# Sums of four steps for the softmax denominators in four more quarters of a decoder layer

## The chip, the cores and the metric

The kernel runs as one program on 1 core of a Trainium2 chip. The metric is the device time of one execution in microseconds (us), lower is better. The kernel before took 1848.51 us (median of 3 runs, 1848.01 to 1848.87).

## What is computed

One post-norm decoder layer in float32 on 2 x 1024 tokens of width 512: linear attention, cross-attention over 2 x 2048 context rows, and a mixture of 8 experts with the 2 best taken per token. The change touches the cross-attention alone:

```python
dots = jnp.einsum('bhnd,bhmd->bhnm', q, k) * SCALE     # 16 heads of 32, n = 1024, m = 2048
attn = jax.nn.softmax(dots, axis=-1)
out = jnp.einsum('bhnm,bhmd->bhnd', attn, v)
```

The kernel computes exp(score - shift), sums its products with v (the numerators) and sums it over m (the denominators), and divides once at the end.

## The kernel before, in words

**Turns, steps, blocks, quarters.** The cross-attention is a loop of 16 turns (0 to 15). A turn is a group of four heads for one half (512) of one batch item's queries. A turn has 16 steps; a step is 128 context rows. Two steps make a block, so a turn has blocks 0 to 7, and four steps make a quarter, so it has quarters 0 to 3 (quarter q is blocks 2q and 2q + 1). In one pass of the inner loop TensorE (PE) computes the eight score products of the next block (`score`, L1446) interleaved with eight products whose maxima are wanted for a later turn (`max_scores`, L1427), then now and then a piece of other work (rows of the output projection, L1258, L1358, routing tables L1258), then the numerators of the current block (`numerators`, L1457: 2 steps x 4 heads, which the trace shows as 16 records, two for each float32 matmul), and last whatever denominator sums are due (`denominators_of`, L1481). In what follows a block's window reaches from the start of its numerators to the start of the next block's numerators, and so holds its numerators, the denominator sums due in it and the score and maximum products that follow.

**The probabilities and how they are summed.** ScalarE (ACT) writes exp of each score into one of nine tiles `probs`, each [128, 4, 512] (L2207). GpSimd (POOL) adds the second step of each block onto the first, one head at a time (`add_head`, L2329, four additions a block). From there are two ways:

- A plain quarter: TensorE multiplies each pair's sum with a matrix of ones as soon as it is due, one block later. That is one sum of four matmuls (8 records) for each block, two for the quarter.
- A quarter by fours: GpSimd issues one accumulating DMA of 1 MB (`add_four`, L2333), which adds the first pair's sum onto the second pair's, and TensorE multiplies only that, four blocks later (three in the quarters of `LAST_BEFORE_PLAIN`). That is one sum of four matmuls for the quarter.

**A visit.** All denominator sums of a turn that are due in the same block make one visit: they accumulate in one PSUM bank, VectorE (DVE) turns the result once (`turn_den`, L1815, a transpose of 128x512) and GpSimd adds the turned column onto `den_s` (`add_den`, L2355 for the first of a turn, L2358 after). So two sums in one visit cost TensorE twice and VectorE and GpSimd once. The visit in which the last step of the turn is summed must be the turn's last; after it come the reciprocal (L1827), a transpose (L1828) and the division on GpSimd (L2367).

The program writes its order out by hand. What is due when is decided here:

```python
if not by_fours(turn, s):
    pending.append((clock + 1, turn, s + 1))
elif s % FOUR == 2:
    fours.append((turn, s + 1))
    pending.append((clock + (3 if (turn, s // FOUR) in LAST_BEFORE_PLAIN else 4), turn, s + 1))
```

`clock` counts blocks. Before the change the quarters by fours are: all four of turns 0 to 6 and 8; the first three of turns 7, 9 and 11; the second and third of turn 10; the first two of turns 13 and 14. Turn 12 has none and turn 15 has none. 47 quarters go by fours and there are 62 visits.

**The order on the other engines.** VectorE takes the maxima of the products of L1427 (`take_max`, L1793, eight a block) in the order in which TensorE makes them, and between them the transposes and the element-wise work of the output rows and the routing (L1870, L1896 to L1982). Maxima, denominator sums and side work take turns in a ring of four PSUM banks, so TensorE can be at most some four products ahead of VectorE. Score products use a ring of three banks which ACT frees. ACT's exp for a step waits for the numerators and for the addition that read the buffer it overwrites: the second tile of a pair five steps later, the first tile thirteen steps later (for a quarter by fours its DMA must have landed by then). On GpSimd the DMA of a quarter stands in the order after the additions of its second block and the divisions that are due, and before the additions of the next block. SyncE issues all loads of keys, queries and values.

Of the kernel before, what the change touches and what calls it, by code (L numbers as in the profile page):

```python
# [20 lines left out]
NG = H // HG  # L21
# [34 lines left out]
TILES_Y = 2  # L56
FOUR = 4

LAST_BEFORE_PLAIN = {(2 * NG - 1, 2), (9, 2), (10, 2), (11, 2)}

LATER_FOURS = {(8, 0), (8, 1), (8, 2), (8, 3), (9, 0), (9, 1), (9, 2), (10, 1), (10, 2), (11, 0), (11, 1), (11, 2),
               (13, 0), (13, 1), (14, 0), (14, 1)}
PARTS = 3
PIECES_Y = B * NT // TILES_Y
HALF_Y = B * NT // 2
# [73 lines left out]
def program(nc, t):  # L139
    ctx = ExitStack()  # L140
    with ctx:
# [178 lines left out]
        def by_fours(t, s):  # L320

            return t * MT + s < B * NG * MT - FOUR or (t, s // FOUR) in LATER_FOURS

# [549 lines left out]
        def add_denominators():  # L873
            while summed:
                t, s = summed.pop(0)
                do("add_den", t, s)
                if s == MT - 1:
                    divisions.append((t, WHOLE))
# [87 lines left out]
        for turn, (n, h) in enumerate(turns):  # L966
            b, g = groups[n]
            stay = stay_of[turn]
            for s in range(0, MT, 2):
# [49 lines left out]
                if not end:  # L1019
# [9 lines left out]
# [3 lines that stand above are left out]
                add_denominators()  # L1032
# [1671 lines left out]
```

## Time and profile before

| | before |
|---|---|
| median of 3 runs (lowest, highest) | 1848.51 us (1848.01, 1848.87) |
| the profiled execution: time of the run | 1852.36 us |
| the profiled execution: span | 1850.6 us |
| TensorE matmul busy | 1824.5 us, 99% |
| VectorE busy | 1275.9 us, 69% |
| ScalarE busy | 879.0 us, 47% |
| GpSimd busy | 845.6 us, 46% |
| mean granted TensorE clock | 0.994 of full speed |

The profiled execution took 1852.36 us, of which the span in the trace is 1850.6 us. Durations are read from that execution. Matmul records overlap, so a busy TensorE is not one that could not be quicker; what a group of matmuls costs is read from the chain of work that ended last, which gives each group the time by which it moves the end. "L1481" is line 1481 of the kernel.

### The profile page before, as it was taken

The numbers are of one execution on the slowest core, as the hardware profiler recorded it, in microseconds if no ns is written. First come the engines' busy times: TensorE is split into PE (matmuls) and PEld (weight loads), VectorE is DVE, ScalarE is ACT, GpSimd is POOL, SyncE is SP. The second block draws the span as 40 slices with busy tenths as digits, with TensorE's granted clock in tenths as the row PEclk, the third lists the DMA queues.
The fourth block names the chain that finished last, engine by engine and source line by source line (L and its number), as shares of the span: only waits on it lengthen the run. The fifth ranks groups of instructions, "written<-read, shape, count | busy, mean of one in ns | idle before, by whom it ended". The sixth has DMA issues, their size and how long they took to land.

```text
span 1850.6 us, 27558 instructions
## 1 busy us (share of the span) xinstructions
PE 1824.5 (99%) x10260; PEld 1275.2 (69%) x10260; DVE 1275.9 (69%) x2350; ACT 879.0 (47%) x1587; POOL 845.6 (46%) x817
## 2 busy tenths in 40 slices
PE   9999999999999999999999999999999999999998
PEld 8786687788655555555555545555459988899986
DVE  6775574268788788888799788779554455554457
ACT  4312322322666566666465556547635333344343
POOL 4002201100598899999687768667202223212232
PEclk9999999999999999999999999999999999999999
DMA  8003534584768586757596556444227766666744
GB/s 291 24 1 119 178 104 172 206 241 152 167 142 183 109 188 143 168 124 170 105 224 146 140 142 148 115 108 110 92 97 222 196 169 153 173 181 177 205 111 157
DMA packets 151286, 280.07 MB, mean 151 GB/s; under 512 B 14288, under 2 KB 50400, under 8 KB 145056
## 3 DMA queue, kind: packets, MB, share of 16 engines
q1 hardware_dynamic: 134896, 205.92, 37.8%
q0 software_dynamic: 16256, 72.39, 19.3%
q8 instruction: 81, 1.33, 0.3%
q14 instruction: 53, 0.43, 0.1%
HBM read 157.63 MB, written 71.60 MB: 124 GB/s over the span
## 4 chain that ended last, share of the span: by engine, by line
PE 87%; DVE 9%; DMA 2%; issue 1%; POOL 0%; ACT 0%; SPq 0%; POOLq 0%; ACTq 0%; DVEq 0%
PE banks L1258 37%; PE banks L1575 12%; PE banks L1446 12%; PE banks L1457 11%; PE banks L1427 11%; DVE max L1793 5%; PE banks L1481 4%; PE banks L1264 1%; DMA k_half<-in_xwk_t 0%; PE banks L1358 0%; DVE den_t L1815 0%; DMA y_rows<-y_nat 0%; POOL x_nat L2340 0%; DMA x_rows<-x_nat 0%; PE banks L1435 0%
## 5 line engine op out<-in xcount | busy, mean ns | idle before, releaser
L2329 POOL TENSOR_TENSOR probs<-probs,probs 128x512 f32<-128x512 f32 x464 | 585.3, 1308 | 185.7 <-PE banks L1457 184.5
L2207 ACT ACTIVATE probs<-banks 128x512 f32<-128x512 f32 x1024 | 518.4, 623 | 285.2 <-PE banks L1446 284.9
L1793 DVE TENSOR_REDUCE max<-banks 128x1 f32<-128x512 f32 x1024 | 625.3, 679 | 39.4 <-PE banks L1427 38.9
L1427 PE MATMUL banks<-k_stack,q_stack 98*128 98x512 f32 x1024 | 401.4, 400 | 3.9 <-DVE max L1793 3.9
L1446 PE MATMUL banks<-q_stack,k_stack 98*128 98x512 f32 x1024 | 404.6, 408 | 0.1
L1446 PEld LDWEIGHTS banks<-q_stack,k_stack 98*128 98x128 f32 x1024 | 191.6, 188 | 152.8 <-issue 103.7
L1457 PE MATMUL banks<-probs,v_grp 128*32 128x512 f32 x2048 | 252.3, 605 | 0.0
L1427 PEld LDWEIGHTS banks<-k_stack,q_stack 98*128 98x128 f32 x1024 | 193.0, 188 | 54.0 <-DVE max L1793 21.1
L1457 PEld LDWEIGHTS banks<-probs,v_grp 128*32 128x32 f32 x2048 | 60.3, 110 | 117.8 <-issue 111.5
L2271 ACT ACTIVATE hid<-banks,b1c 128x640 f32<-128x640 f32 x64 | 50.9, 796 | 189.6 <-PE banks L1575 189.6
L2021 DVE TENSOR_TENSOR hid_lo<-hid,hid_hi 128x640 fp32r<-128x640 f32 x64 | 52.7, 824 | 120.1 <-ACT hid_hi L2276 115.1
L2387 POOL DMA_INDIRECT y_rows<-eo,tok x35 | 60.9, 1739 | 162.1 <-DMA y_rows<-eo,tok 94.0
L2340 POOL TENSOR_TENSOR x_nat<-x_nat,bxo_row 128x512 f32<-128x512 f32 x16 | 21.3, 1358 | 232.7 <-PE banks L1264 232.7
L1258 PE MATMUL banks<-w_hi,hid_lo 128*128 128x512 f32 x320 | 126.5, 395 | 0.0
L1258 PE MATMUL banks<-w_lo,hid_hi 128*128 128x512 f32 x320 | 126.0, 394 | 0.0
L1258 PE MATMUL banks<-w_hi,hid_hi 128*128 128x512 f32 x320 | 125.1, 391 | 0.0
L1575 PE MATMUL banks<-xe_hi,w_hi 128*128 128x320 f32 x512 | 118.7, 309 | 0.0
L1575 PE MATMUL banks<-xe_hi,w_lo 128*128 128x320 f32 x512 | 118.6, 309 | 0.0
L1575 PE MATMUL banks<-xe_lo,w_hi 128*128 128x320 f32 x512 | 118.6, 309 | 0.0
L2378 POOL DMA_INDIRECT xg<-x_rows,tok x40 | 39.2, 981 | 161.7 <-DVE banks L1998 130.8
L1815 DVE STREAM_TRANSPOSE den_t<-banks 128x512 f32<-128x512 f32 x62 | 44.3, 715 | 75.9 <-PE banks L1481 71.8
L1481 PE MATMUL banks<-probs,ones 128*32 128x512 f32 x656 | 87.2, 603 | 2.1 <-DVE max L1793 2.0
(272 smaller groups left out, 2789.6 us busy)
## 6 DMA issues: line engine op xcount, KB each, us to landing
probs<-probs POOLq DMA_DIRECT2D x47, 1024.0 KB, 10.6
k_stack<-k_parts SPq DMA_DIRECT2D x144, 256.0 KB, 5.5
w_raw<-in_w_rows SPq DMA_DIRECT2D x8, 2048.0 KB, 9.9
w_raw<-in_L_ffn_w SPq DMA_DIRECT2D x8, 2048.0 KB, 8.5
q_stack<-q_parts SPq DMA_DIRECT2D x48, 256.0 KB
v_grp<-v_rows SPq DMA_DIRECT2D x48, 256.0 KB, 3.8
slot_rows<-xg SPq DMA_DIRECT2D x35, 256.0 KB, 2.1
xg<-slot_rows SPq DMA_DIRECT2D x140, 64.0 KB, 8.1
```

The lines of the kernel that those rows point to most:

```text
L1258: done = nc.tensor.matmul(out, lhsT, rhs, start=start and n == 0, stop=stop and n == len(operands) - 1)
L1427: nc.tensor.matmul(out, queries_of(t)[:, j, tile_of(k)], keys_of(t)[0:STK + SHIFT, j, mc * HALF:(mc + 1) * HALF], start=True, stop=True) \
L1446: nc.tensor.matmul(out, keys_of(t)[0:STK + SHIFT, j, tile_of(s)], queries_of(t)[:, j, :], start=True, stop=True).then_inc(scored.sem, 1)
L1457: done = nc.tensor.matmul(bank(NUM)[j * DH:(j + 1) * DH, :], v_grp[:, s, j * DH:(j + 1) * DH], probs_of(t, s)[:, j, :], start=s == 0, stop ...
L1481: done = nc.tensor.matmul(out[j * DH:(j + 1) * DH, :], ones[:, 0:DH], tile[:, j, :], start=begun and n == 0, stop=n == len(tiles) - 1 and ...
L1575: done = nc.tensor.matmul(both[:, h, 0:HC], w, x[:, h * HC:(h + 1) * HC], start=n == 0, stop=n == len(terms) - 1)
L1793: V.reduce_max(max4[:, tiles_of(t), :, :][:, k, j, mc:mc + 1], bank(bank_of["max", t, mc, k, j]), AX.X) \
L2021: V.tensor_tensor(hid_lo[:, f, :], hid[f % 2][:, :], hid_hi[:, f, :].bitcast(F32), ALU.subtract) \
L2207: S.activation(probs_of(t, s)[:, j, :], bank(bank_of["score", t, s, j]), ACT.Exp, scale=SCALE) \
L2271: S.activation(hid[f % 2][:, :].rearrange("p (h n) -> p h n", h=2), pairs[first][:, :, 0:HC], ACT.Gelu, bias=b1c[:, e, f:f + 1]).then_inc( ...
L2329: G.tensor_tensor(a[:, j, :], a[:, j, :], b[:, j, :], ALU.add).then_inc(pair_added.sem, 1)
L2387: G.indirect_dma_start(out=y_rows, in_=eo[turn % EO][:, :], in_offset=None, compute_op=ALU.add, out_offset=bass.IndirectOffsetOnAxis(ap=to ...
```

## The change

Four quarters join the set that goes by fours: (10, 0), (12, 0), (12, 1) and (13, 2). Since quarter 3 of turn 13 stays plain, (13, 2) also joins the set whose sum is due one block earlier, so that it shares the turn's last visit.

```diff
-LAST_BEFORE_PLAIN = {(2 * NG - 1, 2), (9, 2), (10, 2), (11, 2)}
+LAST_BEFORE_PLAIN = {(2 * NG - 1, 2), (9, 2), (10, 2), (11, 2), (13, 2)}
 
-LATER_FOURS = {(8, 0), (8, 1), (8, 2), (8, 3), (9, 0), (9, 1), (9, 2), (10, 1), (10, 2), (11, 0), (11, 1), (11, 2),
-               (13, 0), (13, 1), (14, 0), (14, 1)}
+LATER_FOURS = {(8, 0), (8, 1), (8, 2), (8, 3), (9, 0), (9, 1), (9, 2), (10, 0), (10, 1), (10, 2), (11, 0), (11, 1), (11, 2),
+               (12, 0), (12, 1), (13, 0), (13, 1), (13, 2), (14, 0), (14, 1)}
```

The denominator sums due in each block follow from the rule above (q0 is quarter 0; a quarter that is plain has an a for its first block's sum and a b for its second's; x8 is one sum, x16 two; blocks not named hold none):

| turn | before | after |
|---|---|---|
| 10 | block 1: q0a x8; 2: q0b x8; 7: q1 and q3a x16; block 0 of turn 11: q2 and q3b x16 | block 5: q0 x8; 7: x16; block 0 of turn 11: x16 |
| 12 | blocks 1 to 6: q0a, q0b, q1a, q1b, q2a, q2b, x8 each; 7: q3a x8; block 0 of turn 13: q3b x8 | block 5: q0 and q2a x16; 6: q2b x8; 7: q1 and q3a x16; block 0 of turn 13: x8 |
| 13 | block 5: q0 and q2a x16; 6: q2b x8; 7: q1 and q3a x16; block 0 of turn 14: q3b x8 | block 5: q0 x8; 6: none; 7: x16; block 0 of turn 14: q2 and q3b x16 |

## Rows read from the trace of the kernel before

**Rows 1.** Page, busy time of the engines, and chain that ended last by engine.

```profile
PE 1824.5 (99%) x10260; PEld 1275.2 (69%) x10260; DVE 1275.9 (69%) x2350; ACT 879.0 (47%) x1587; POOL 845.6 (46%) x817
...
PE 87%; DVE 9%; DMA 2%; issue 1%; POOL 0%; ACT 0%; SPq 0%; POOLq 0%; ACTq 0%; DVEq 0%
```

**Rows 2.** Windows of six blocks: length, busy time of each engine, clock, DMA share, GB/s.

```profile
1024.07:1030.67 6.60, 6.60 (x42) 3.61 (x41) 5.48 (x10) 4.01 (x9) 5.99 (x8) 1.00 0.83 219
...
1141.95:1149.14 7.19, 7.19 (x41) 3.29 (x41) 7.12 (x15) 4.62 (x10) 5.95 (x7) 1.00 0.15 36
1149.14:1156.56 7.42, 7.13 (x41) 3.34 (x40) 7.35 (x14) 4.02 (x9) 6.23 (x8) 1.00 0.47 108
1156.56:1166.33 9.77, 9.27 (x58) 5.12 (x57) 9.46 (x18) 4.48 (x10) 5.56 (x7) 1.00 0.22 49
1166.33:1172.96 6.63, 6.63 (x42) 3.61 (x41) 4.03 (x8) 3.38 (x8) 5.22 (x5) 1.00 0.38 87
...
1232.48:1238.22 5.74, 5.74 (x37) 3.33 (x29) 4.60 (x9) 3.38 (x8) 5.29 (x5) 1.00 1.03 227
```

**Rows 3.** Chain that ended last in turns 10, 12 and 13: start, us, what.

```profile
1025.99 0.86 PE banks L1481 x8
...
1070.56 1.72 PE banks L1481 x16
...
1168.25 0.86 PE banks L1481 x8
...
1240.33 1.72 PE banks L1481 x16
...
1247.79 0.86 PE banks L1481 x8
```

**Rows 4.** The same chain in blocks 1 to 3 of turn 12.

```profile
1145.69 0.60 DVE den_t L1815
...
1153.09 0.62 DVE den_t L1815
...
1160.52 0.04 DVE top L1800
...
1160.66 0.70 DVE den_t L1815
...
1164.38 2.01 PE banks L1258 x16
```

**Rows 5.** Timeline of block 3 of turn 12, on ACT and PE.

```profile
1160.91 3.99 ACT L2207 ACTIVATE probs<-banks 128x512 f32<-128x512 f32 x8
...
1163.83 0.46 PE L1427 MATMUL banks<-k_stack,q_stack 98*128 98x512 f32 x1
```

**Rows 6.** Chain in block 7 of turn 13 and block 0 of turn 14, with one DVE row.

```profile
1253.60 2.47 DVE L1793 TENSOR_REDUCE max<-banks 128x1 f32<-128x512 f32 x4
...
1254.37 1.89 PE banks L1481 x16
...
1263.02 0.90 PE banks L1481 x8
1264.10 0.72 DVE den_t L1815
```

**Rows 7.** The DMA of four steps, all 47: min/median/max ns on POOL; us to landing.

```profile
L2333 POOL DMA_DIRECT2D probs<-probs x47: 807/872/942, 494.4 to 1290.3; - x47
...
DMA to landing us min/median/max: 6.9/10.6/14.7
```

**Rows 8.** POOL and the chain around quarter 2 of turns 11 and 13.

```profile
1120.22 0.87 POOL L2333 DMA_DIRECT2D probs<-probs  x1 [0.25 <-POOL den_s L2355]
...
1136.42 1.76 PE banks L1481 x16
...
1244.61 0.20 POOL L2355 COPY den_s<-den_t 128x16 f32<-128x16 f32 x1
```

**Rows 9.** DVE's routing addition with two inputs in SBUF: min/median/max ns.

```profile
L1904 DVE TENSOR_TENSOR rt_lg<-rt_lg,router_bias x4: 191/1232/1241, 953.3 to 1373.1; 128x32 f32<-128x32 f32 x4
```

## The prediction

> **What bounds the kernel now.** I read the page first: TensorE is busy 99% of the span, and the chain of work that ended last is 87% TensorE, 9% VectorE [rows 1]. So work taken off TensorE counts in most places and not in all, and the question is what bounds each block in which a sum is removed. For that I cut turns 10, 12 and 13 into blocks by the starts of their numerators and asked for the windows of the blocks, then for the chain over the same stretches. The granted clock is 1.00 in all these windows [rows 2], the full 2.4 GHz level, and TensorE has no idle stretch in them that the change would lengthen, so no term for the clock is set.
>
> Three kinds of block are seen [rows 2]. The bare one, 1232.48 to 1238.22, holds eight scores, eight maxima and the numerators and no sum: 5.74 us, TensorE busy throughout, VectorE 4.60. The one with one sum, 1024.07 to 1030.67, is 6.60, that is 5.74 + 0.86; and the chain gives such a sum 0.86 and a double one 1.72 [rows 3]. There TensorE sets the time. The third kind is blocks 1 to 3 of turn 12, from 1141.95 to 1166.33: VectorE is busy 7.12 of 7.19, 7.35 of 7.42 and 9.46 of 9.77, because the routing work of other rows falls there, and the chain runs through VectorE, its transposes included [rows 4].
>
> **The change part by part.** A quarter by fours has one sum in place of two. Four quarters: four sums fewer, 4 x 0.86 = 3.44 us of TensorE. By the table of sums due, 12 sums' places change and the visits fall from 4 to 3 in turn 10, from 8 to 4 in turn 12 and from 4 to 3 in turn 13: six transposes fewer, 6 x 0.72 = 4.3 us of VectorE [rows 6], and six small additions fewer on GpSimd (0.2 each, as the last row of [rows 8]). Added are four accumulating DMAs, 0.87 us of issue on GpSimd and 10.6 us to landing each [rows 7]. The gain has to be placed block by block.
>
> Turn 10: blocks 1 and 2 lose a sum each, block 5 gains one. TensorE sets all three. Would VectorE take over? In block 2 it is busy 5.48, less 0.72 for its transpose is 4.76, under 5.74 [rows 2]: no. So -0.86 - 0.86 + 0.86 = **-0.86**.
>
> Turn 12, blocks 1 to 3: three sums and three transposes go, but VectorE sets the time, so the sums are worth nothing and the transposes what the chain gives them: 0.60 and 0.62 in blocks 1 and 2 [rows 4]. In block 3 the transpose is 0.70 of chain, but another limit lies close beneath: the exps of that block start at 1160.91, just after VectorE's top (1160.52), since ACT's copy of that maximum stands ahead of them in its order, and with three score banks TensorE's last maximum product starts only at 1163.83 [rows 5] and would end about 1164.1, against 1164.38 at which the tables' products start [rows 4]. That chain is not shortened by the transpose behind it. It leaves about 0.3. Stretch: -0.60 - 0.62 - 0.31 = -1.53. Block 4 (6.63, one sum, VectorE 4.03 [rows 2]) is TensorE's: -0.86. Blocks 5 and 7 gain a sum: +1.72. Together **-0.67**, against -1.72 by TensorE's count.
>
> Turn 13: block 5 goes from a double sum to one and block 6 from one to none: -1.72 [rows 3]. In block 7 the double sum stays, at 1254.37; its bank is the one read by the fifth maximum, which VectorE finishes at 1253.60 + 0.61 = 1254.2 [rows 6]. VectorE came to it through the steps of a reciprocal root that it runs between its maxima, and it moves earlier with the transpose taken out, by some 1.3 to 1.6, while TensorE would be there 1.72 earlier: I put 0.25 of waiting there. In block 0 of turn 14 one sum becomes two: +0.86; but its transpose began at 1264.10, 0.18 after the sum's end at 1263.92, because VectorE was still at routing work [rows 6]. That wait is covered now: -0.18. Together -1.72 + 0.25 + 0.86 - 0.18 = **-0.79**. From that transpose on the chain is VectorE's for some 13 us, so its start is what counts.
>
> GpSimd: the four issues of 0.87 stand ahead of the next block's pair additions. The tightest place is block 2 of turn 12: GpSimd is busy 6.23 [rows 2], + 0.87 - 0.22 = 6.9 in a block that shrinks to 6.8. Its additions would lag by about 0.1 us, and ACT needs them only in the next block's exps. Price taken: 0; what hides it is about half a block of slack, and without that cover it would cost at most its own 0.87 once. SyncE's queue is not passed by anything: the DMAs are GpSimd's.
>
> The landings: three of the new quarters have over 20 us from issue to sum. The tightest is (13, 2). GpSimd frees itself at 1244.8 [rows 8], and the sum falls after the numerators of block 0 of turn 14, which start 1.44 earlier than now: about 1261.5. That is 16.7 us, against 14.7 for the slowest of 47 landings [rows 7]. The like case exists: quarter 2 of turn 11 is issued at 1120.22 and summed at 1136.42, 16.2 us later, and TensorE goes straight from its numerators into that sum [rows 8]. Price 0.
>
> A term that I can bound only is the meeting of VectorE and GpSimd. VectorE's small routing addition takes 0.19 us at its fastest and 1.23 in the median of four [rows 9], an excess of 1.04, near the length of one of GpSimd's additions. As the blocks move against each other, such meetings come and go in the stretches where VectorE sets the time. I take 0 for it, as the nearest rows show it on both sides of the change alike, and keep -1.0 and +2.0 (two places at which one may appear, at 1.04 each) for the range. The Trainium skill has a rule for it (SBUF — State Buffer, the section "SBUF: two separate sides"): VectorE and GpSimd share a pair of ports under an exclusive lock, so an operation of VectorE with two SBUF inputs waits for a whole GpSimd instruction. The trace agrees, 0.19 against 1.23 us; by that rule the gain in turn 12 could be lost to the new order, and it is the rival of the lock below.
>
> Sum: -0.86 - 0.67 - 0.79 = -2.32 us. After turn 14 nothing differs, and the end of the kernel is one chain of TensorE, routing and expert products, so the gain reaches the end. The profiled execution of 1852.36 (span 1850.6) would be 1850.04. It stood 3.85 above the median of the timed runs, 1848.51; the same difference off that median gives 1846.19, rounded **1846.2 us**, -0.13%. A measurement of this kernel tells about 0.2%, 3.7 us, from no change.
>
> **The rivals.**
>
> *TensorE's price in full.* VectorE turns out to have room where I saw it bind, with 4.3 us of transposes gone, and all four sums count: -3.44, 1845.1. For it: TensorE's 99%. Against: VectorE's 7.12 of 7.19 in turn 12. Chance 0.15.
>
> *The lock.* In the stretch of turn 12, or at the routing of turns 13 and 14, one or two operations of VectorE now meet GpSimd's additions: -2.32 + 1.04 = -1.3 with one, -0.2 with two, 1847.2 to 1848.3. For it: in blocks 1 and 2 of turn 12 VectorE's table work would come up to 1.2 us earlier against GpSimd's additions, which follow the numerators. Against: it can as well be lifted. Chance 0.22.
>
> *A large gain.* The full price and a meeting lifted: -3.44 - 1.04 = -4.5, 1844.0. Chance 0.07.
>
> *Slower: the landing of (13, 2).* Its DMA lands later than 16.7 us after issue and TensorE waits in block 0 of turn 14. It decides the sign from 16.7 + 2.3 = 19.0 us on; at 20.3 the time is +1.3, 1849.8. For it: one quarter more lies in flight beside the keys' and queries' loads. Against: 14.7 is the maximum of 47. Chance 0.06.
>
> That the change doesn't do what it says is no rival: both sets are constants that the plan reads.
>
> **How the numbers follow.** My case, -1.6 to -3.1, gets 0.50 with 1846.2 in its middle. The range takes it, the full price and nearly all of the lock, with some 0.4 us on either side for the spread of runs: 1844.5 to 1848.5. Faster by over 0.2% (under 1844.8) needs the large gain or the lucky edge of the full price: 0.09. Slower by over 0.2% (over 1852.2) needs a landing 6 us too late or several meetings: 0.03. The rest, 0.88, is within 0.2%.
>
> **What would show it.** In the profile after: 51 DMAs of four steps, 56 transposes L1815, 624 records of L1481; blocks 1 and 2 of turn 10 at 5.74 to 5.8 us and block 5 0.86 longer; blocks 1 to 3 of turn 12 at about 6.6, 6.8 and 9.5, still full on VectorE; a span of about 1848.3. Blocks 1 to 3 of turn 12 at 5.8, 5.8 and 7.8 would prove the first rival and me wrong about VectorE; a routing operation of 1.2 us where there was none the second; a wait of L1481 for a DMA in block 0 of turn 14 the fourth. A gain above 3.7 us or a loss would show that the method of adding blocks misses a coupling between them.

## The result, and the profile after

The changed kernel took 1857.03 us (median of 20 runs, 1850.94 to 1865.98) against 1848.97 us of the kernel before (20 runs, 1845.54 to 1852.50): ratio 1.0047, 95% interval 1.0037 to 1.0056. It is slower, where the prediction had 1846.2 and a range of 1844.5 to 1848.5. The profiled execution took 1855.75 us, span 1854.0, against 1852.36 and 1850.6.

Busy time by engine and the chain by engine, from the page of the changed kernel:

```profile
PE 1817.0 (98%) x10228; PEld 1275.3 (69%) x10228; DVE 1284.1 (69%) x2344; ACT 879.8 (47%) x1587; POOL 846.9 (46%) x815
...
PE 86%; DVE 10%; DMA 2%; issue 1%; POOL 1%; ACT 0%; SPq 0%; DVEq 0%; POOLq 0%; ACTq 0%
```

Against [rows 1], TensorE has 32 records fewer and VectorE 6. Yet VectorE is busy 8.2 us longer, though six transposes of 0.72 us are gone. That is the first sign: some of its operations took much longer. ("VectorE busy" holds the time in which an operation has begun and waits.)

The counts came as forecast (51 DMAs, 56 transposes, 624 records), and the landings did not suffer. Lines L2333, L1815 and L1481 of the changed kernel:

```profile
L2333 POOL DMA_DIRECT2D probs<-probs x51: 817/871/947, 494.2 to 1297.2; - x51
...
DMA to landing us min/median/max: 6.9/10.2/14.7
...
L1815 DVE STREAM_TRANSPOSE den_t<-banks x56: 704/717/718, 513.7 to 1365.4; 128x512 f32<-128x512 f32 x56
...
L1481 PE MATMUL banks<-probs,ones x624: 592/592/617, 512.4 to 1364.8; 128*32 128x512 f32 x156
```

Blocks 1 and 2 of turn 10, block 2 of turn 12 and block 2 of turn 14 of the changed kernel (windows: length, busy time of PE, PEld, DVE, ACT, POOL, granted clock, DMA share, GB/s):

```profile
1014.34:1020.09 5.75, 5.75 (x34) 3.34 (x33) 4.23 (x9) 3.35 (x7) 4.51 (x4) 1.00 0.40 107
1020.09:1025.83 5.74, 5.74 (x33) 3.34 (x32) 4.87 (x9) 4.02 (x9) 5.74 (x8) 1.00 1.04 281
1144.63:1159.30 14.67, 9.04 (x34) 5.40 (x33) 14.53 (x18) 4.82 (x9) 7.16 (x9) 0.65 0.59 126
1276.52:1290.61 14.09, 8.33 (x38) 5.41 (x37) 13.77 (x17) 4.73 (x9) 7.09 (x9) 0.76 0.37 74
```

Turn 10 is as predicted: 5.75 and 5.74 where [rows 2] has 6.60 for the second. But block 2 of turn 12 takes 14.67 us in place of 7.42 [rows 2], and block 2 of turn 14 takes 14.09 in place of 9.33. Block by block, the profiled executions differ so:

| | before | after | measured | predicted |
|---|---|---|---|---|
| turn 10, blocks 1, 2, 5 | 6.62, 6.60, 9.64 | 5.75, 5.74, 10.49 | -0.88 | -0.86 |
| turn 12, block 1 | 7.19 | 6.59 | -0.60 | -0.60 |
| turn 12, block 2 | 7.42 | 14.67 | +7.25 | -0.62 |
| turn 12, block 3 | 9.77 | 7.70 | -2.07 | -0.31 |
| turn 12, blocks 4, 5, 7 | 6.63, 6.81, 10.24 | 5.78, 7.63, 11.10 | +0.83 | +0.86 |
| turn 13, blocks 5, 6 | 7.65, 6.58 | 6.81, 6.07 | -1.35 | -1.72 |
| turn 13, block 7 | 8.64 | 9.93 | +1.29 | +0.25 |
| turn 14, blocks 0, 1 | 6.62, 6.74 | 7.45, 6.55 | +0.64 | +0.68 |
| turn 14, block 2 | 9.33 | 14.09 | +4.76 | 0 |

Blocks 1 to 3 of turn 12 go together, since VectorE's second table pass (L1970 to L1976), which ran over the start of block 3 before, now lies inside the long block 2: together +4.58 us where I had -1.53. Of the other blocks from turn 10 on, all but two are as before to 0.04 us. The table adds up to +9.9 us and the spans differ by 3.4 only, because the profiled execution of before had stretches at half the clock of its own: one ahead of turn 10 (600.62 to 607.45, granted clock 0.50; in the changed kernel turn 10 starts 3.1 us earlier), and one in block 7 of turn 14 and block 0 of turn 15 (10.17 and 7.19 us against 9.29 and 4.81 after). A third lies inside block 2 of turn 14 (1279.88 to 1283.29), so its 9.33 us are more than usual; with quarter (10, 0), (12, 0) or (12, 1) alone by fours this block took 8.66 to 8.67. What happened in block 2 of turn 12 is in the timelines of the changed kernel, VectorE first, then GpSimd, then TensorE (start, us, instruction, in brackets the idle time before it and its releaser):

```profile
1145.61 0.31 DVE L1972 TENSOR_TENSOR hot_col<-col_no,slot_col 128x160 f32<-128x160 int32 x1
1145.96 5.51 DVE L1974 TENSOR_TENSOR hot_col<-hot_col,weight 128x160 f32<-128x160 f32 x1
1151.51 0.46 DVE L1976 TENSOR_TENSOR hot_col<-hot_col,token_no 128x160 f32<-128x160 f32 x1
```

```profile
1145.09 0.84 POOL L2333 DMA_DIRECT2D probs<-probs  x1
1145.89 4.99 POOL L2329 TENSOR_TENSOR probs<-probs,probs 128x512 f32<-128x512 f32 x4
1150.78 1.00 POOL L2367 TENSOR_TENSOR heads_t<-num_c,den_c 128x128 f32<-128x128 f32 x2
```

```profile
1146.49 0.50 PE L1446 MATMUL banks<-q_stack,k_stack 98*128 98x512 f32 x1
1152.62 0.80 PE L1427 MATMUL banks<-k_stack,q_stack 98*128 98x512 f32 x1 [5.63 <-DVE max L1793]
1153.22 0.63 PE L1446 MATMUL banks<-q_stack,k_stack 98*128 98x512 f32 x1
...
1158.34 0.63 PE L1446 MATMUL banks<-q_stack,k_stack 98*128 98x512 f32 x1
```

VectorE's L1974, an operation of 0.32 us where nothing is in its way (the row behind this paragraph, from the kernel before), comes 0.07 us after the first of GpSimd's four additions and ends 5.51 us later, when all four and the first of two divisions are over. The maxima stand behind it, so TensorE waits 5.63 us for a bank. And then TensorE runs on at 0.43 us from one product to the next, where the bare block of [rows 2] leaves (5.74 - 1.92) / 16 = 0.24, 1.92 being its numerators' row: the granted clock of that window is 0.65, so a good part of it was at the lower of the two levels, 1.2 GHz. From 1152.62 to 1159.30 it makes 15 products in 6.7 us, where 3.6 is usual (15 x 0.24). The wait costs twice.

```profile
1150.01 0.32 DVE L1974 TENSOR_TENSOR hot_col<-hot_col,weight 128x160 f32<-128x160 f32 x1
```

Turn 14 has the same with the third operation of L1928, on VectorE and on GpSimd of the changed kernel:

```profile
1277.42 6.22 DVE L1928 TENSOR_TENSOR before<-before,rt_ms 128x8 f32<-128x8 f32 x3
```

```profile
1277.00 0.85 POOL L2333 DMA_DIRECT2D probs<-probs  x1
1277.77 5.03 POOL L2329 TENSOR_TENSOR probs<-probs,probs 128x512 f32<-128x512 f32 x4
```

In both places the DMA issue of four steps ends as the additions begin (1277.00 + 0.85 = 1277.85, additions from 1277.77): no gap. The kernel before has that DMA of turn 14 too, but there a gap of 0.12 us follows (1274.74 + 0.85 = 1275.59, additions from 1275.71), and VectorE's L1933 waits for one addition, 1.24 us. The additions wait for the first step's numerators and start some 1.25 us after the block does, before and after (1274.45 to 1275.71, 1276.52 to 1277.77); what moved is the issue, which starts 0.29 us into the block before and 0.48 us after, and so eats the gap. GpSimd and VectorE of the kernel before:

```profile
1274.74 0.85 POOL L2333 DMA_DIRECT2D probs<-probs  x1
1275.71 4.98 POOL L2329 TENSOR_TENSOR probs<-probs,probs 128x512 f32<-128x512 f32 x4
```

```profile
1275.76 1.24 DVE L1933 TENSOR_TENSOR before<-before,rt_ms 128x8 f32<-128x8 f32 x1
```

Theory of the port: a two-input operation of VectorE (two inputs in SBUF) that comes at the additions waits for one of them as a rule, but for the whole burst when a DMA issue of GpSimd ends straight into it. Rivals: the removed sums cost by themselves; the burst alone, without the DMA, does it; the DMA does it, gap or no gap.

### The profile page after: what moved, and what is told of

Same layout as the page of the kernel before. It is cut to its first block, busy times and chain, and to the rows that moved or that the text cites. A ratio compares the mean times of both kernels' runs of the same rounds, so it can differ in the third digit from the quotient of the medians.

```text
span 1854.0 us, 27469 instructions
## 1 busy us (share of the span) xinstructions
PE 1817.0 (98%) x10228; PEld 1275.3 (69%) x10228; DVE 1284.1 (69%) x2344; ACT 879.8 (47%) x1587; POOL 846.9 (46%) x815
## 4 chain that ended last, share of the span: by engine, by line
PE 86%; DVE 10%; DMA 2%; issue 1%; POOL 1%; ACT 0%; SPq 0%; DVEq 0%; POOLq 0%; ACTq 0%
PE banks L1258 36%; PE banks L1575 12%; PE banks L1446 12%; PE banks L1457 11%; PE banks L1427 11%; DVE max L1793 5%; PE banks L1481 4%; DMA raw<-in_x_t 1%; PE banks L1264 1%; PE banks L1358 1%; DMA k_half<-in_xwk_t 0%; DVE before L1928 0%; DVE den_t L1815 0%; DVE hot_col L1974 0%; POOL x_nat L2340 0%
## 5 line engine op out<-in xcount | busy, mean ns | idle before, releaser
L1781 DVE TENSOR_TENSOR out_lo<-banks,out_hi 128x512 fp32r<-128x512 f32 x48 | 33.0, 690 | 79.0 <-ACT out_hi L2152 78.8
L1815 DVE STREAM_TRANSPOSE den_t<-banks 128x512 f32<-128x512 f32 x56 | 40.1, 717 | 68.8 <-PE banks L1481 63.9
```

## The experiments

All ratios are against runs of the kernel before on the same chip, with 95% intervals.

### One quarter at a time

```diff
-               (13, 0), (13, 1), (14, 0), (14, 1)}
+               (13, 0), (13, 1), (14, 0), (14, 1), (12, 0)}     # or (10, 0), (12, 1), (13, 2)
```

For (13, 2) the quarter is in the other set too, as in the change.

> Only quarter (10, 0) goes by fours in addition. Its DMA is issued in block 2 of turn 10, where VectorE has no routing work. Theory of the port (GpSimd's divisions, DMA issue and four additions run without a gap, and a two-input VectorE operation that comes to them waits for nearly the whole burst, 5 to 6 us): no such meeting here, so -0.9 us (blocks 1 and 2 at 5.75, block 5 0.86 longer). Rival, that merging or removing sums costs through the banks or the visits: slower by 1 us or more here too.

> Only quarter (12, 0). Theory of the port: block 2 of turn 12 has L1974 at about 5.5 us in place of 0.33 and is some 7 us longer, net +4 to +7 us. Rival, that the shift of the blocks by all four quarters together makes the meeting: L1974 stays at 0.33 to 1.2 us and the time is within 1 us of before.

> Only quarter (12, 1). Its DMA is issued in block 4 of turn 12, after the table work, so the theory of the port gives no wait there: blocks 3 and 4 shorter, block 7 0.86 longer, -0.5 to -1 us. If the time is worse by over 2 us, the cost lies with the later quarters of turn 12 and not with GpSimd's burst.

> Only quarter (13, 2). The long wait of 5.8 us on L1928 in block 2 of turn 14 stood in the changed kernel beside a DMA that the kernel before has too (14, 0). If the change of (13, 2) causes it (its double sum in block 0 of turn 14 holds VectorE back by 0.86 us against GpSimd), it is here as well: +3 to +6 us. If it came from the shift by the other quarters, or by chance of the execution, L1928 is short here: -0.8 us.

| quarter | median us | before | ratio | mean granted clock, median of runs (before 0.998) |
|---|---|---|---|---|
| (10, 0) | 1846.34 | 1847.10 | 0.9996 (0.9985 to 1.0007) | 0.998 |
| (12, 1) | 1846.39 | 1847.10 | 0.9998 (0.9990 to 1.0007) | 0.998 |
| (12, 0) | 1852.93 | 1847.10 | 1.0036 (1.0023 to 1.0049) | 0.9945 |
| (13, 2) | 1854.03 | 1847.10 | 1.0035 (1.0022 to 1.0047) | 0.995 |

Two quarters do no harm and two cost over 0.3% each. With (12, 0) alone VectorE shows the same row, 0.09 us after the additions begin, and block 2 of turn 12 takes 13.69 us:

```profile
1149.52 5.91 DVE L1974 TENSOR_TENSOR hot_col<-hot_col,weight 128x160 f32<-128x160 f32 x1
```

```profile
1148.65 0.82 POOL L2333 DMA_DIRECT2D probs<-probs  x1
1149.43 5.00 POOL L2329 TENSOR_TENSOR probs<-probs,probs 128x512 f32<-128x512 f32 x4
```

With (13, 2) alone it is L1928 in block 2 of turn 14, 6.21 us for its three, and the block takes 14.05. There the DMA is one that the kernel before had. What (13, 2) changed is the order of events: its double sum holds VectorE up in block 0, and in block 2 GpSimd's DMA issue starts 0.48 us after the numerators in place of 0.29, so that it ends only as the numerators let the additions go. Quarters (10, 0) and (12, 1) have sums removed and merged as well and cost nothing, so removing a sum does not cost in itself, which settles the first rival.

### The DMA behind the additions

```diff
+DMA_AFTER = {(12, 4)}                    # (14, 4) with (13, 2); both with all four
-                    while fours:
+                    while fours and (turn, s) not in DMA_AFTER:
                         do("add_four", *fours.pop())
...
                             do("add_head", turn, s + 1, j)
+                    while fours:
+                        do("add_four", *fours.pop())
```

(12, 4) is a turn and a step: the additions in question are those of block 2. In the two runs "twice" the two divisions ahead of the additions are done two times each, with a wait for the first between:

```diff
+                if (t, k) in {(11, 0), (11, 1)}:          # (13, 0), (13, 1) with (13, 2)
+                    step.settle(G.tensor_tensor(heads_t[:, g, h * HALF + k * P:h * HALF + (k + 1) * P],
+                                                num_c[:, tile_of(k)], den_c[:, tile_of(k)], ALU.mult))
```

> Quarter (12, 0) by fours as in the run with that quarter alone, but in block 2 of turn 12 GpSimd issues the DMA behind its four additions, not ahead of them. The additions then wait for TensorE's numerators, as before the change. Theory of the port: L1974 waits for at most one addition (up to 1.3 us), the 6.5 us are gone, and the time is -0.5 to -1.5 us against before. Rival, that the missing sum and transpose alone move VectorE's table work into the additions: L1974 or L1976 is again at over 5 us and the time stays near +6.

> As the last, DMA behind the additions, but the two divisions ahead of them (L2367 for the first two pieces of turn 11) are each done twice, so GpSimd comes to the additions about as late as with the DMA issue ahead, and finds the numerators ready. If a gapless burst of GpSimd is what keeps VectorE out, one two-input operation waits 5 us or more again and the time is +4 to +7. If it takes the DMA's own descriptors, no operation waits for more than one addition and the time is near that of the last run.

> Quarter (13, 2) alone by fours, and in block 2 of turn 14 the DMA of (14, 0), which the kernel before has too, is issued behind the additions. Theory of the port: the 6.2 us of L1928 shrink to under 2 us and the time is -0.5 to -2 us. If L1928 still takes over 5 us, the DMA ahead of the additions is not what matters.

> All four quarters, with the DMAs of (12, 0) and (14, 0) behind the additions of block 2 of their turns. Theory of the port: no operation of VectorE waits for more than about one addition at a time, and the sum of the prediction comes true, -2 to -4 us, faster than both kernels. If the time is over 1850, another cost of the change is still missing from the account.

> Quarter (13, 2) by fours, the DMA of (14, 0) behind the additions, and the two divisions ahead of them done twice each, so that GpSimd runs divisions and additions without a gap when VectorE's L1928 and L1933 come, but without a DMA issue among them. If a gapless burst keeps VectorE out for its whole length, one of them takes 4 us or more and block 2 of turn 14 is over 12.5 us. If it takes a DMA issue straight ahead of the additions, each waits for at most one or two GpSimd instructions (up to 1.5 us) and the block stays at 8 to 11 us.

| | median us | before | ratio | turn 12 blocks 2, 3 | turn 14 block 2 |
|---|---|---|---|---|---|
| late, (12, 0) | 1849.14 | 1847.89 | 1.0005 (0.9995 to 1.0015) | 9.90, 8.68 | 7.37 |
| late twice, (12, 0) | 1852.76 | 1847.89 | 1.0022 (1.0010 to 1.0034) | 7.44, 14.25 | 7.33 |
| late, (13, 2) | 1850.27 | 1847.89 | 1.0015 (1.0006 to 1.0025) | 8.57, 9.29 | 10.17 |
| late, all four | 1849.46 | 1847.89 | 1.0016 (1.0003 to 1.0029) | 10.06, 8.08 | 10.28 |
| late twice, (13, 2) | 1846.56 | 1847.83 | 0.9993 (0.9982 to 1.0005) | 8.55, 9.31 | 9.03 |

No two-input operation of VectorE in turns 10 to 13 and the first three blocks of turn 14 takes over 1.7 us in any of these. Most of the loss is gone in three of them, all of it in the last, and about a third of it in "late twice, (12, 0)". But the expected gain did not come: with (12, 0) three operations now wait for an addition or two divisions each (1.62, 1.37 and 1.27 us), and the clock falls for a while. That part of the expectations was wrong.

The wait itself is told by "late, (12, 0)": L1974 (here L1978) comes to the additions at the same distance as in the run of that quarter above, 0.09 us, only without a DMA issue ahead, and takes 1.37 us in place of 5.91. VectorE, then GpSimd:

```profile
1148.09 1.37 DVE L1978 TENSOR_TENSOR hot_col<-hot_col,weight 128x160 f32<-128x160 f32 x1
```

```profile
1148.00 5.13 POOL L2333 TENSOR_TENSOR probs<-probs,probs 128x512 f32<-128x512 f32 x4 [0.73 <-PE banks L1461]
```

The third operation of L1928 (here L1932) does the same in "late, (13, 2)": 0.09 us behind the start of the additions, 1.21 us in place of 5.81. But in both GpSimd had stood idle for 0.7 us ahead of the additions, so these two don't tell a gapless burst from a DMA issue.

The run "late twice, (13, 2)" decides between burst and DMA. Its VectorE and GpSimd in block 2 of turn 14:

```profile
1272.06 1.20 DVE L1937 TENSOR_TENSOR before<-before,rt_ms 128x8 f32<-128x8 f32 x1
```

```profile
1271.53 0.47 POOL L2374 TENSOR_TENSOR heads_t<-num_c,den_c 128x128 f32<-128x128 f32 x1
1271.96 4.98 POOL L2333 TENSOR_TENSOR probs<-probs,probs 128x512 f32<-128x512 f32 x4
```

(Lines have moved by four to seven in this kernel.) The division runs straight into the additions, VectorE comes 0.10 us into the first, and it waits for that one alone. A gapless burst of additions is not enough; the DMA issue right ahead is what the long waits have in common. In the run "late twice, (12, 0)" VectorE passed between the doubled divisions and never met the burst; block 3 grew in its place, through the second table pass (1.39, 1.27 and 1.27 us) and a half-clock stretch.

The 17 traces (before, after and the 15 experiments) hold more such meetings than these. A two-input operation of VectorE comes 0 to 0.2 us behind the start of an addition that directly follows a DMA issue with no gap in four places, and these are the four long waits, 5.5 to 5.9 us. With a gap of 0.07 to 0.17 us it does so in 19 places (L1889 and L1933, whatever their line in the run), and takes 1.1 to 1.3 us in each. That settles the third rival: the DMA without the closed gap does not do it. Two places limit the theory. In "late twice, (12, 0)" the late DMA issue (1155.38, 0.84 us) runs straight into two divisions and then four additions; VectorE's L1976, which comes 0.04 us before the first division, takes 1.39 us, through both divisions and no addition. And shorter instructions of GpSimd can keep VectorE out one behind the other without a DMA: the 1.62 us above hold the last 0.2 us of an addition and two divisions.

### A gap between the DMA and the additions

The four additions of that block now wait for the numerators of the block's second step, not of its first, and so GpSimd stands idle behind the DMA issue. `(12, 5)` is turn 12, step 5, the second of block 2; "hold more" has (12, 7) of block 3 as well.

```diff
-                pool.wait_ge(*num_summed[t, s - 1])
+                pool.wait_ge(*num_summed[t, s if (t, s) in {(12, 5), (14, 5)} else s - 1])
```

> Quarter (12, 0) alone by fours, its DMA issued ahead of the additions as in the change; only in block 2 of turn 12 GpSimd's additions wait for the second step's numerators in place of the first's, so that GpSimd stands idle between the DMA issue and the additions (a gap of 0.2 us or more in place of none) while VectorE does its table work. Theory of the port: L1974 takes 0.3 to 1.3 us, block 2 is 6.7 to 7.9 us, the time is -0.5 to -1.5 us against before. If the DMA issue itself is what keeps VectorE out, gap or not, L1974 or L1976 is at over 4 us again.

> Quarter (13, 2) alone by fours; in block 2 of turn 14 the additions wait for the second step's numerators. Theory of the port: L1928 and L1933 are done before the additions begin, block 2 of turn 14 is 7.3 to 8.7 us in place of 14.1, and the time is -0.5 to -2 us. Rival as in the last.

> The changed kernel with both holds. Theory of the port with the clock's share (waits of TensorE bring half-clock stretches, so with the waits the dips go): the blocks add up to what the prediction summed, -2 to -4 us against before, and the granted clock is that of before, 0.997 or more. If it is over 1848, the dips or waits stay though the long waits are gone.

> All four quarters, with holds in block 2 and also in block 3 of turn 12 and block 2 of turn 14. With the hold in block 2 alone VectorE's second table pass met the additions of block 3 (13.8 us for that block). Theory of the port: with the second hold block 3 falls to 8.5 to 10.5 us and the time to -1 to -4 us. If block 3 stays over 12 us, something other than the additions holds VectorE there.

| | median us | before | ratio | turn 12 blocks 2, 3 | turn 14 block 2 |
|---|---|---|---|---|---|
| hold, (12, 0) | 1851.60 | 1847.43 | 1.0024 (1.0013 to 1.0034) | 7.28, 12.93 | 7.37 |
| hold, (13, 2) | 1845.86 | 1847.43 | 0.9991 (0.9983 to 1.0000) | 7.42, 9.76 | 7.83 |
| hold, all four | 1849.59 | 1847.43 | 1.0009 (1.0000 to 1.0017) | 7.29, 13.79 | 7.81 |
| hold more, all four | 1849.57 | 1847.83 | 1.0010 (0.9995 to 1.0024) | 6.84, 14.91 | 7.81 |

For (13, 2) the hold does what was expected: the same quarter that cost 0.35% now costs nothing (0.9991, with 1.0000 at the edge of the interval), and block 2 of turn 14 is 7.83 us. VectorE is through with L1928 and L1933 (0.57 us for three, 0.17) before the additions begin, partly during the DMA issue itself, so the issue alone doesn't hold it up. GpSimd of that run:

```profile
1273.30 0.85 POOL L2333 DMA_DIRECT2D probs<-probs  x1
1274.89 5.02 POOL L2329 TENSOR_TENSOR probs<-probs,probs 128x512 f32<-128x512 f32 x4 [0.74 <-PE banks L1457]
```

In turn 12 the hold clears block 2, but VectorE's second table pass then meets divisions and additions in block 3 (12.93 us), and the time is 0.24% worse, where 0.5 to 1.5 us of gain was expected. With all four quarters the expected gain and clock (0.997 or more) did not come either: 1.0009, and a median of the mean granted clock of 0.9945 against 0.997. Holding the additions of block 3 too was a miss: it took 14.91 us. The rows of that run tell how a small wait grows. VectorE (L1970, 0.68 us when nothing is in its way; here it is out for the rest of an addition and for two divisions, until 1151.86), then TensorE, then the block's window:

```profile
1150.17 2.24 DVE L1970 TENSOR_TENSOR hot_row<-lane_no,slot_row 128x512 f32<-128x512 int32 x1
```

```profile
1154.95 0.50 PE L1427 MATMUL banks<-k_stack,q_stack 98*128 98x512 f32 x1 [1.86 <-DVE max L1793]
...
1157.75 0.80 PE L1446 MATMUL banks<-q_stack,k_stack 98*128 98x512 f32 x1 [1.10 <-ACT probs L2207]
1158.34 0.63 PE L1427 MATMUL banks<-k_stack,q_stack 98*128 98x512 f32 x1
```

```profile
1150.74:1165.65 14.91, 11.95 (x49) 8.22 (x49) 11.36 (x17) 4.92 (x10) 7.22 (x9) 0.72 0.64 127
```

Some 3 us of waits are followed by products at 0.43 us again, granted clock 0.72 in the window. So the expectation of 8.5 to 10.5 us was wrong because it left out the clock and the divisions; the additions alone were not in the way for over 1.3 us at a time.

### Without the quarter (12, 0)

`two_quarters` has (10, 0) and (12, 1); `three_hold` has (13, 2) as well and the hold of step 5 of turn 14.

> Quarters (10, 0) and (12, 1) by fours, the two that do no harm alone. If costs and gains are local they add up: -1.2 to -1.7 us. If the shift of the blocks against each other is what makes meetings anywhere, one of the blocks 2 of turns 12 or 14 grows by over 2 us.

> Quarters (10, 0), (12, 1) and (13, 2) by fours, without (12, 0), and the hold in block 2 of turn 14 (additions wait for the second step's numerators). From the single runs (-0.7, -0.7, -1.6): -2.5 to -4 us against before, faster than both kernels, granted clock 0.997 or more.

`two_quarters`: 1844.51 against 1847.43, 0.9986 (0.9975 to 0.9996). `three_hold`: 1845.09 against 1847.83, 0.9984 (0.9973 to 0.9995). Both beat both kernels by a little: -2.9 us by the medians where -1.2 to -1.7 was expected (inside the interval, -0.7 to -4.6), and -2.7 where -2.5 to -4 was. Between the two the intervals don't tell, so the third quarter is not shown to gain anything. In `three_hold` no operation of VectorE near the changed blocks takes over 1.24 us.

## Why the prediction was wrong

**The counting was right.** Turn 10, block 1 of turn 12, the exchanges of sums in blocks 4, 5 and 7 of turn 12 and the start of turn 14 came within 0.04 us of the working. In block 6 of turn 13 I had 0.86 of gain and 0.51 came, since VectorE with its root steps bounds it. With (13, 2) alone block 7 of turn 13 takes 8.75 us and with the three other single quarters 8.47 to 8.48, so the 0.25 of waiting there was right; in the changed kernel one more meeting (L1889, 1.28 us) came on top.

**The step that failed** is the term "that I can bound only", the meeting of VectorE and GpSimd, with the step on GpSimd's issues that should have fed it. I priced an issue at its own 0.87 us and found it covered by slack, asking only whether its additions come late for ACT. What it did was another thing: it closed the gap ahead of the additions. And I bounded a meeting by the longest that [rows 9] hold, 1.04 us of excess. A meeting at the closed gap cost VectorE 5.2 to 5.7 us, and the block 5.4 us (14.09 against the 8.67 of an undisturbed execution) to 7.9 us (14.67 against the 6.80 that I had worked out). The bound was set from a trace in which the case did not occur; the rival of the lock had the right place and a price of a fifth. Block 2 of turn 14, where the second long wait came, lay behind the last window that I had read and counted as unchanged.

The Trainium skill's rule (SBUF — State Buffer, section "SBUF: two separate sides") has the loser block until the whole instruction of the other is done. The one-addition waits agree, 1.2 us. The long ones don't fit one instruction: L1974 stayed out for four additions and a division, 5.51 us, so here the measurement goes further than the page. Why a DMA issue with no gap behind it keeps VectorE out so long is not shown by any run here, nor is it that a port is what they wait for. What is shown is that each of the four long waits (two in the changed kernel, one in each of the runs with (12, 0) and (13, 2) alone) came with it, that a gapless burst without it gave 1.20 us, and a DMA with a gap of 0.07 to 0.17 us gave 1.1 to 1.3 us, 19 times.

**The clock** was left out on the ground that TensorE had no idle stretch that the change would lengthen. That was so only as long as the first step held. In block 2 of turn 12 it took some 3 us of the loss (6.7 in place of 3.6 for 15 products). From turn 10 to turn 14 all twelve waits of TensorE of 1.86 us or more, over all traces, had products at 1.2 GHz behind them, and the medians of the mean granted clock, 0.9945 and 0.995 in the two harmful single runs against 0.998, show it in the timed runs too. The Trainium skill's page TensorE: Matmul & The Clock Gate (section "HAM oscillation — how this bites in real kernels") says that waits between matmuls throw TensorE to half rate and that the work behind them pays as well; the trace agrees, with 6.7 us for 15 products in place of 3.6.

**The other rivals.** TensorE's price in full did not come: block 1 of turn 12 took 6.57 us or more and block 2 at least 6.84 in every run. Block 3 did fall to 7.70 in the changed kernel, but only because the table pass lay in the long block before it. The landing was no cause: 14.7 us at most, as before.

The two harmful quarters cost +5.8 and +6.9 us alone and the harmless ones -0.8 and -0.7; their sum, +11.3, is above the +8.1 of all four. Four intervals of about 0.1% (2 us) each lie in that sum, so the difference may be noise.

## What to carry to other kernels

When work is added to a GpSimd that seems to have slack, look at what stands behind it on GpSimd and what VectorE does at that time: two-input operations of VectorE wait for GpSimd, and in this kernel what counted was the gap that was lost, not the busy time. Where VectorE feeds TensorE's banks, price such a wait together with the slower clock behind it. Try sites of a repeated change one at a time: here two of four were harmless, and a one-word wait made a third harmless.

## What the runs showed of the hardware

- A VectorE operation of 0.17 to 0.32 us took 5.5 to 5.9 us when it came 0.04 to 0.09 us after GpSimd had begun four additions straight behind a DMA issue, and 1.2 us when a gap of 0.12 us lay between, at the same distance. During a DMA issue alone such operations took their 0.17 to 0.19 us, and four gapless additions without it held one up for 1.2 us.
- TensorE's products of 98x512 were 0.24 us apart at the full level and 0.43 after waits of 5.6 us, and also after two waits of 1.9 and 1.1 us with 2.8 us between their ends.
- The same code falls into one of two lengths in places where such meetings are a matter of 0.1 us: block 2 of turn 12, not touched by the edit, was 7.42 to 7.45 us in one group of runs and 8.55 to 8.57 in another. In the first VectorE's L1976 came at the start of GpSimd's addition or up to 0.02 us before it and took 0.32 to 0.33 us, in the second up to 0.02 us behind its start and took 1.43 to 1.44.
